# A planned two-layer transformer kernel: margins in the plan's delays and a new table of offsets

## The reference, cut to what matters

```
h = layernorm(x) * (1 + ca) + sa
x = x + ga * attention(h)          # 16 heads of 8 features; layer 1 is causal
h = layernorm(x) * (1 + cb) + sb
x = x + gb * experts(h)            # 8 experts, each position uses its 2 best
# layer 0: experts swiglu with 352 hidden features (and one shared expert for all)
# layer 1: relu(h @ W1[e])**2 @ W2[e], 128 hidden features
```

## Time and profile before

| | |
|---|---|
| median of 3 runs | 1109.6 us (1108.39 to 1110.48) |
| profiled execution, its own time | 1111.04 us |
| its span, first to last instruction | 1109.3 us |
| mean granted TensorE clock | 0.949 of full speed |
| PE, DVE, ACT, POOL busy | 1005.7, 856.3, 726.3, 440.8 us |
| PE matmuls, DVE, ACT, POOL instructions | 8319, 1752, 1145, 536 |

### The profile page before, as it was taken

How to read it: one execution, slowest core, us unless ns; L and a number is a source line. 1 busy time by engine, 2 the same in 40 slices (tenths; PEclk the granted TensorE clock), 3 DMA queues, 4 the chain that set the end, 5 groups by cost and what they waited for, 6 DMA issues and landing times.

```text
span 1109.3 us, 22600 instructions
## 1 busy us (share of the span) xinstructions
PE 1005.7 (91%) x8319; PEld 535.2 (48%) x8319; DVE 856.3 (77%) x1752; ACT 726.3 (65%) x1145; POOL 440.8 (40%) x536
## 2 busy tenths in 40 slices
PE   5679799889999999989999999989999999999995
PEld 3221222223555453645556666556675554445564
DVE  5798889878989778798866888789876576885464
ACT  4257577585576775667685675755765687777763
POOL 5030012253014423820454453565332377715563
PEclk8659889897999999999999999999999999999998
DMA  5743335253547684755568666787776647411100
GB/s 165 191 126 76 110 81 141 63 190 90 169 161 216 204 232 140 218 153 172 167 197 251 206 211 200 253 210 221 240 232 187 202 127 208 121 51 34 41 10 20
DMA packets 120030, 174.43 MB, mean 157 GB/s; under 512 B 19912, under 2 KB 83784, under 8 KB 119920
## 3 DMA queue, kind: packets, MB, share of 16 engines
q1 hardware_dynamic: 113584, 159.60, 48.6%
q0 software_dynamic: 5760, 12.59, 4.0%
q10 hardware_dynamic: 576, 0.79, 0.2%
HBM read 114.21 MB, written 58.59 MB: 156 GB/s over the span
## 4 chain that ended last, share of the span: by engine, by line
PE 40%; DVE 20%; DMA 16%; issue 10%; POOL 7%; ACT 5%; SPq 1%; POOLq 0%; DVEq 0%; ACTq 0%
DVE nm L1033 12%; PE ps L825 9%; DMA gr<-d_y,pos 7%; PE ps L899 6%; PE ps L808 5%; PE ps L786 4%; PE ps L921 3%; DMA d_h<-r,pos 3%; ACT ES L1381 3%; PE ps L763 2%; PE ps L945 2%; POOL gr L1609 2%; DMA d_h<-hx,pos 2%; PE ps L938 1%; POOL ya L1630 1%
## 5 line engine op out<-in xcount | busy, mean ns | idle before, releaser
L1033 DVE TENSOR_REDUCE nm<-ps 128x2 f32<-128x1024 f32 (+3 forms) x512 | 502.8, 1017 | 97.0 <-PE ps L786 48.8
L1381 ACT ACTIVATE ES<-ps 128x1024 f32<-128x1024 f32 (+1 forms) x448 | 418.9, 963 | 122.4 <-PE ps L808 75.5
L825 PE MATMUL ps<-ES,VS 128*9 128x512 f32 (+3 forms) x2048 | 225.7, 530 | 1.2 <-DVE rj L1158 0.5
L786 PE MATMUL ps<-KS,QS 48*128 48x512 bf16 (+3 forms) x1024 | 176.2, 365 | 34.9 <-DVE nm L1033 27.5
L808 PE MATMUL ps<-QS,KS 51*128 51x512 bf16 (+3 forms) x1024 | 171.0, 354 | 16.7 <-ACT ES L1381 8.2
L899 PE MATMUL ps<-hsT,wst 128*128 128x128 f32 x1104 | 157.3, 285 | 3.5 <-issue 2.6
L899 PEld LDWEIGHTS ps<-hsT,wst 128*128 128x128 f32 x1104 | 134.8, 191 | 43.7 <-issue 39.1
L786 PEld LDWEIGHTS ps<-KS,QS 48*128 48x128 bf16 x1024 | 49.4, 95 | 157.3 <-DVE nm L1033 69.2
L808 PEld LDWEIGHTS ps<-QS,KS 51*128 51x128 bf16 x1024 | 49.4, 94 | 147.8 <-issue 50.9
L1609 POOL DMA_INDIRECT gr<-d_y,pos x80 | 83.4, 1042 | 84.1 <-DMA gr<-d_y,pos 47.6
L1539 POOL TENSOR_TENSOR nmp<-nmr,nmp 32x128 bf16<-32x128 f32 x32 | 13.5, 420 | 193.0 <-ACT nmp L1373 192.4
(11 more groups left out here) (206 smaller groups left out, 1491.8 us busy)
## 6 DMA issues: line engine op xcount, KB each, us to landing
wst<-we SPq DMA_DIRECT2D x92, 576.0 KB
d_u<-US SPq DMA_DIRECT2D x60, 256.0 KB
KS<-d_k SPq DMA_DIRECT2D x62, 192.0 KB
QS<-d_q SPq DMA_DIRECT2D x62, 192.0 KB
hs<-d_h SPq DMA_DIRECT2D x25, 256.0 KB
d_y<-ys SPq DMA_DIRECT2D x25, 256.0 KB
d_q<-sp SPq DMA_DIRECT2D x16, 384.0 KB
d_k<-sp SPq DMA_DIRECT2D x16, 384.0 KB
```

The lines of the kernel that those rows point to most:

```text
L786: mm = eng.matmul(psum[:, bank[u][a], c:c + n], QS[m][r:r + KA, pr, 128 * t1:128 * t1 + 128], KS[m][r:r + KA, pr, 0:n], start=True, stop=i ...
L825: mm = eng.matmul(psum[32 * a:32 * a + 9, b, q0:S], VS[i % 3][:, j1, 4 * g + a, :], ES[(2 * EXP[i, g, j] + a // 2) % NES][:, a % 2, c:c + ...
L1033: ins = eng.tensor_reduce(nm[f][:, :].rearrange("p (a c) -> p a c", a=2)[:, :, 4 * pr + t1], ps2("score", i, f, pr, t)[:, :, c:c + n], AX. ...
L1381: eng.activation(ES[(2 * n + pp) % NES][:, :, 0:w], ps2("bscore", i, f, g, j, pp)[:, :, 0:w], ACT.Exp, scale=SC1 if i >= NB else SC0).then ...
```

## The change

Nothing that is computed changes, and each engine issues the same work. Three things change in the plan. Every lag gets an addition: 0.6 (`LATER`) for transfers and all steps whose lag is 1.0 or more, 0.05 (`SPARE`) for the other steps of PE, DVE and ACT. The tables SHIFT, LATE, LAST and NUDGE get new numbers. Together they make another order and other bank choices.

```
+LATER, SPARE = 0.6, 0.05
     def add(self, engine, key, weight, urgency, after=(), lag=None, mode="full", opens=0, closes=()):
         lag = self.LAG[engine] if lag is None else lag
+        if lag >= 1.0 or key[0] in self.MOVES:
+            lag += LATER
+        elif engine in ("PE", "DVE", "ACT"):
+            lag += SPARE
-    "g": [-10.16, -6.15, -14.08, ...
+    "g": [-15.06, -10.11, -15.22, ...
...
```

More of the change, by code:

```diff
@@ L77 @@
-LAST = {"bscore": -0.02, "c": 13.05, "d": 0.58, "early": 2.99, "expo": -8.28, "f": -3.24, "g": 7.45, "ld": 5.89, "m": 9.88, "max": -12.3, "p": -0.93, "pv": 1.54, "r": -6.13, "rowmax": -4.86, "rr": -4.9, "s": -7.69, "score": -0.01, "stack": 4.54, "t": 1.7, "u": 5.02, "v": -8.29, "w": -8.74, "x": 2.33}
+SHIFT = {"bscore": -0.08, "c": -29.77, "d": 7.85, "early": -15.24, "expo": -3.98, "f": -1.03, "g": -9.54, "ld": -13.03, "m": 9.98, "max": 2.14, "p": -0.3, "pv": 0.21, "r": 7.54, "rr": -0.06, "s": 0.8, "score": -0.08, "stack": 4.67, "t": 0.18, "u": 3.59, "v": -2.86, "w": 0.42, "x": 1.09}
@@ new lines @@
+LATE = {"c": 17.24, "d": 5.93, "early": -14.17, "expo": 9.81, "f": -1.07, "g": 12.86, "ld": 15.38, "m": 2.2, "max": -19.05, "p": 0.01, "r": 16.1, "rowmax": 0.68, "rr": -15.57, "s": -13.83, "score": 0.02, "stack": -9.77, "t": 0.54, "u": 14.14, "v": -3.47, "w": -34.23, "x": 12.68}
+LAST = {"bscore": -0.02, "c": 3.66, "d": -0.64, "early": -0.11, "expo": -13.05, "f": -15.15, "g": -5.54, "ld": -9.51, "m": 16.29, "max": -19.33, "p": -2.66, "pv": 3.05, "r": 5.18, "rowmax": 6.85, "rr": -8.42, "s": -6.65, "score": -0.01, "stack": 10.28, "t": 1.97, "u": 12.23, "v": 3.0, "w": -5.37, "x": 7.25}
```

10 lines of the change are left out of this document (4 added, 6 removed), and 18 rows, old and new, of the table NUDGE.

## The result

The kernel after takes 1090.0 us, the median of four runs (1089.7 to 1092.9); the kernel before took 1109.0 in the same comparison (1104.4 to 1110.5, four runs). The ratio is 0.984, with a 95% interval of 0.981 to 0.988. A copy of the kernel after in a later comparison gave 0.9865 (0.984 to 0.989). So the change makes the kernel some 14 to 19 us faster. The prediction, 1105.4 with a range from 1096, had the direction and missed the size.

The account below looks back on a forecast made before the run. PE was taken as the bound from 277 to 1053 us, after DVE's maxima, then both together. Terms -2.0 + 1.0 - 1.0 - 2.2 + 0 = -4.2 gave 1106.8 for the profiled execution, 1105.4 as forecast; range 1096 to 1116.

Parts of the forecast that it names:

- Step 5: Everything else: several hundred exchanged neighbours not followed, taken as 0, with -6.5 and +7.5 us kept for the range.
- Step 1: Start: six gate instructions leave DVE's way, so second reduction and first exponential come earlier; -2.0 us.
- Step 4: Group 4's first tiles, near 851.88: fourteen more steps ahead of the transpose remove PE's wait; -2.2 us.
- Step 2: Pass 1: the gates' DVE work moved between its maxima, close to the layer-1 gates, partly hidden; +1.0 us.
- Step 3: Pass 1's first bscore: more PE work stands in the gap where PE waited 1.47 us for QS; -1.0 us.
- the clearly faster one: From 57 to 277 us, shorter waits for maxima and a higher clock, 6.5 us more gained: 1099 us; chance 0.14.
- The slower rival: New bank choices lengthen waits for the exponentials' banks after 277 us by 7 to 12: 1112 to 1117 us; chance 0.28.
- a sign of being wrong: Waits for ES at L808 and L786 (L813 and L791 after) rising above 15 us, from 11.7 before.
- The second reduction: Sign at the start on DVE: it begins within 0.2 us of the end of the first reduction.
- PE's wait for QS<-d_m near 112: Sign at pass 1's first bscore: this wait falls below 1 us.
- PE's idle time from 57 us to the tail: Sign: PE's idle time from the start of the exponentials to the tail falls below 66 us.
- The wait at group 4's first x_turn: Sign for group 4's first tiles: no wait over 0.5 us there.

Follow-up runs that it names:

- after_again: The kernel after, unchanged, run again in a later comparison: 1092.9 us, ratio 0.9865 to the kernel before.
- early_a: The kernel after with before's order and lags up to the first PV group of pass 0: 1089.2 us, ratio 0.986 to before.
- early_c: The kernel after with before's order and lags up to the first PV group of pass 0's last quarter: 1086.5 us, ratio 0.983 to before.
- start_only: The kernel before with only the start's moves (layer 0's gates later, second score block ahead of the projections): 1117.4 us, ratio 1.013.
- late_new_more: Before's order up to pass 3's third PV group (PV step 3,2), after's order from there, a repeated run: 1096.8 us, ratio 0.991 to before.

## Why the prediction was wrong

The step that failed is the fifth, which put everything not followed at 0: the order behind pass 3 alone gives 9 to 10 us. Beside it the sum had no term for the clock, whose falls from 110 to 280 us cost 12 us less. Steps 1 and 4 failed too, with less at stake, and both on SP's list. In order:

**Step 1, the start, -2.0.** DVE's part held, the way from it to the first exponential did not. Two executions must be compared in which the clock fell alike before the first reduction: before with 35.02 and after_again with 35.09. DVE of after_again, then its PE and ACT at the end of this half:

```profile
35.09 2.36 DVE L1038 TENSOR_REDUCE nm<-ps 128x2 f32<-128x1024 f32 x2 [4.20 <-PE ps L791]
38.02 4.62 DVE L1038 TENSOR_REDUCE nm<-ps 128x2 f32<-128x1024 f32 x4 [0.58 <-PE ps L791]
```

```profile
65.41 0.61 PE L813 MATMUL ps<-QS,KS 51*128 51x512 bf16 x2 [0.89 <-DMA QS<-d_m]
```

```profile
66.06 1.02 ACT L1386 ACTIVATE ES<-ps 128x1024 f32<-128x1024 f32 x1 [0.17 <-PE ps L813]
```

The first two reductions stand together. The third starts at 38.02, where the second of before stood at 38.31, so DVE is one reduction and 0.29 us ahead, 1.4 us instead of 2.0, since the third block was late by 0.58 and not by the 0.1 worked out. POOL's last piece of the maxima is 1.4 us earlier too (57.53 against 58.93). There it stops, on SP. Its rows in before, then in after_again:

```profile
59.43 0.34 SPq L1717 DMA_DIRECT2D d_m<-nmp  x1
...
62.57 0.56 SPq L1722 DMA_DIRECT2D QS<-d_m  x2
```

```profile
59.15 0.37 SPq L1722 DMA_DIRECT2D d_m<-nmp  x1
...
63.06 0.56 SPq L1727 DMA_DIRECT2D QS<-d_m  x2
```

Three loads (bos, cs and fs) now stand right ahead of the store and are issued from 57.57 to 59.04, where before they stood ahead of the stores of q and k and were out by 53.2. So the store of the maxima goes out 0.3 us earlier and not 1.4, and the load behind it 0.5 later than in before. The first bscore starts at 65.41, where before it was 65.40, and the first exponential shows 0.35 (66.06 against 66.41). From the first reduction to the first exponential it is 31.39 us in before, 30.97 in after_again and 30.52 in after: 0.4 to 0.9 of the 2.0. The step that failed in step 1 is the path from the last maximum to the exponential, which I took to pass on all that DVE gained. That the first exponential was at 62.21 in the profile of after is nearly all the earlier first reduction of that execution (31.69), which is clock.

**Step 2, +1.0.** Put back inside the new order (early_a, 112.7 at 45 units, against 112.2 of after_again), steps 1 and 2 together are worth -0.5 at most, for early_a's clock also stayed down 3.4 us longer in this stretch. -1.0 had been forecast. What neither step held was the 2.8 us lost in the same piece to exchanges that I hadn't followed.

**Step 3, -1.0.** PE's wait for QS<-d_m fell from 2.1 to 0.4 us in all, so the mechanism was right and the size too small: it left out the clock. The two waits of the earlier trace rows, 2.26 us, and 3.2 us lost at half clock behind them went together. The 25 units of work behind 45 take 4.5 us less (47.9 to 43.4). A part of that is the next fall, which is shorter by 3.4 us in after (10.2 to 6.8) and so cost 1.7 less; in early_c it is 10.2 as in before. So this place is worth some 3 to 4 us, where -1.0 was put.

**Step 4, -2.2.** It failed. Fourteen steps more stand ahead of the first x_turn, and PE still waits 1.94 us (1.56 in after_again), where it was 2.18:

```profile
845.70 1.12 PE L895 MATMUL ps<-ident,hs 128*128 128x128 f32 x4 [1.94 <-DMA hs<-d_h]
```

The chain of after ahead of it:

```profile
836.25 0.48 SPq L1714
...
838.30 0.36 SPq L1676
...
838.70 6.96 DMA hs<-d_h
845.70 1.12 PE ps L895 x4
```

I had counted PE's steps and not SP's, as in step 1. The load stood behind the four issues that bring K and Q of a later pass, which wait for PE's last bscore of an earlier one, and took 6.96 us to land where it took 4.03 before. I had read that the consumer moved back, and not that the queue of its load did too.

**Step 5, everything else, 0.** This is the term that puts the forecast out of its range. I had bounded it by the best and the worst idle share of the middle, kept half of each, and let the ends cancel. The new order behind pass 3 gives 9 to 10 us alone (0.990 and 0.991), and 13.5 in the profile (P3 to P5), 9.3 of it idle time. The full lower bound of 13 us of idle time, worked out and then halved, would have held the 9.3. It would not have held the time: 1105.4 less 13 is 1092.4, and 1090.0 was measured. The rest is the clock, for which the sum had no term: it is priced in a rival alone, at 6.5 us, and the falls in P2 cost 12 us less after. The halving assumed that the exchanges were independent of each other; halves that give nothing and together give 10 us show that they are not.

**The range.** Its lower end doesn't follow from its own terms. 1105.4 less 6.5 and less half of 0.6 is 1098.6, not 1096; and the bounds of steps 1 to 4 (-2.15, 0, -1.47, -2.18) add up to -5.8, which is 1.6 below the -4.2 and not 0.6. The measured time lies below either end.

**The rivals.** The one that got near was the clearly faster one, 1099 at a chance of 0.14: the clock in P2 went from 0.88 to 0.95. Its reason was half right, for the idle time there rose by 3.7 us instead of falling. In P2 it was not how long PE stood in all that counted, but where and behind what the clock fell. The slower rival's mechanism did not happen where it was priced. The waits for ES at these two lines did go from 11.7 to 17.2 us, above the 15 that I had called a sign of being wrong, but the rise lies ahead of 277 us (7.2 to 13.5). Behind it, where PE is the bound and the rival had added 7 to 12 us, they fell, from 4.6 to 3.6. A sum over the whole program was the wrong sign to watch.

**The signs.** The second reduction stands right behind the first, PE's wait for QS<-d_m near 112 is gone, and PE's idle time from 57 us to the tail is 61.6 us, below the 66 named (66.4 before). The wait at group 4's first x_turn, which was to be below 0.5 us, stayed. The first exponential at 62.21 looked like more than the forecast 64.4 and was the clock of one execution.

What stays open: which exchanges from pass 3 on make the 10 us. Halves of them give nothing, so a single place on one side of pass 8 is unlikely, unless the seams hid it; and the test with slowed landings gave no support to the margins as the cause. That the chain lost its indexed gathers (DMA 16% to 3%, 4% in after_again; 6% in the spliced kernel that keeps the gain, 8% and 13% in the halves) goes with the gain, but early_c is the fastest with 10%, so it isn't a measure of it.

## What to carry to other kernels

When two orders of the same work are compared, cut both traces at equal work and split each part into busy and idle time: it showed in one table how much of the gain was clock. A wait on TensorE can cost more than its length, since the clock may fall behind it: the 1.47 us at 114.64 brought 3.2 more. The length of one wait doesn't tell, so read the granted clock behind it, and in more than one execution. When a consumer is moved back, follow the list of the engine that issues its transfer too; here SP's list took back most of step 1 and nearly all of step 4. Don't halve the bound of hundreds of exchanges because they should cancel: an order found by search is one thing, and neither its parts nor its offsets keep their worth apart.

## What the runs showed of the hardware

- The same lists gave 108.2 and 112.2 us up to the same work at the start, by the moments at which the clock fell and rose in the first 80 us; the spans differ by 3.5 us. The Trainium skill, in TensorE: Matmul & The Clock Gate (Part 1), says that the slow phase at a kernel's start varies from run to run, and that its penalty is under 1% of a typical kernel. The trace agrees that it varies: the difference of 3.5 in 1090 us is 0.3%. The penalty itself no run here sets apart. The difference is as large as an effect that one may want to read from two profiles.
- Doubling the score matmuls while VectorE set the pace (PE busy 14.18 of 19 us in place of 9.56) raised the mean clock there by 0.05 and no more.
- One PSUM bank pair handed to and fro between TensorE and VectorE gives a maximum each 1.93 us (start_only); with two pairs in turn it is 1.135 (before).
- The clock fell behind one wait of 1.47 us, and behind waits of 0.89, 0.52 and 0.90 us close together; behind one of 2.24 us it fell in after and did not in late_new_more.
- A load of row tiles that took 4.03 us to land took 6.96 in the new order, right behind four issues of other loads.
